# Attention block with row maxima from half-precision q and k, and the projected chunk ahead of the two weighings of its pair of steps

## The chip, the cores and the metric

The kernel runs on one core of a Trainium2 chip. The metric is the device time of one execution in microseconds (us); the median of the runs counts. The engines are TensorE (PE; its weight loads have a row of their own, PEld), VectorE (DVE), ScalarE (ACT), GpSimd (POOL) and SyncE (SP, which here only issues DMAs).

## The reference, cut to what matters

Input x is 2 x 2048 x 256, with 16 heads of 64. Each half is a residual around two layer norms.

```
x = x + layernorm(attn(layernorm(x)))     # q,k,v = x@Wq+bq, x@Wk+bk, x@Wv+bv
                                          # softmax(q.k^T / 8) @ v, @ Wo + bo, add, layernorm, gamma, beta
x = x + layernorm(ffn(layernorm(x)))      # silu(x@wg^T) * (x@wu^T) @ wd^T, weights scaled by 1/127
```

All of it is in float32. The softmax subtracts each query's largest score before the exponential; any number near that maximum gives the same quotient, since it divides out.

## The kernel before, in words

Float32 accuracy comes from splitting a number into a high part and the rest, and multiplying the parts. The operands of the projections and the scores are of the type fp32r, a four-byte form that TensorE takes in one pass; those of the weighing are f16.

The attention part handles two batches of 16 heads. For each (batch, head) there are 4 blocks of 512 queries (`NB`) and 16 tiles of 128 keys (`KT`), so 64 steps a head (`STEPS`), 2048 in all. A step t on TensorE is written out in `head` of the TensorE program and does, in this order:

- **max_tile** (L726 to L736): one product of 128 queries by 512 keys into one of two banks of `ps_aux`, for a block of queries two blocks ahead, so that in steps 32 to 63 it works for the next head. It uses `q_hilo` and `k_hihi`, 128 rows deep. The query is the stationary operand; it takes every fourth column of `qA`, that is one element in 16 bytes. VectorE reads the bank with `reduce_max` (L562, `maximum`) and thereby frees it; TensorE may not write a bank before (`used`, a list of two entries in TensorE's program, holds what each bank waits for).
- **score** (L738 to L747), for step t + 6: two products into a ring of four banks, `ps_score`. The second, 65 rows deep, also subtracts the maximum. ScalarE then computes the exponential of the bank twice (L513, L514), once to f32 and once to f16.
- **weigh** (L749 to L772), after each odd step for the last two steps: 8 short f16 products a step into `ps_ctx`, with the probabilities as the stationary operand. They need the rest `p_l` = `p_f` - `p_h`, made by VectorE in steps with t % 8 in (1, 3, 5) (`low`, L579) and by GpSimd in the others (L442).
- **project** (L713 to L724), at steps 35, 41, 51 and 57: q and k of the head after next, 512 tokens at a time, in 6 products into a bank of `ps_aux`. It stands between the two weighings of its pair. ScalarE copies the bank to `qk_new` after the exponential of step t + 6 (`take_chunk`, L466), VectorE rounds that to `hi_st` at step t + 4 (`high_chunk`, L554), GpSimd makes the rest `lo_st` after step t + 6 (`low_chunk`, L424). The two-tiles-later max_tile waits for ScalarE's copy, because it takes the same bank.

Per block VectorE also reads the sums (L585, L587), divides (L593), reduces the maxima to a row (L565) and negates it (L571); per head it splits the projection's weights at step 24 (`split_w`, L541 to L545). When the four chunks are there, SP's `fill` copies them by six DMAs from `hi_st` and `lo_st` to the operands of the head after (L342). It is issued at the start of the head before the one that uses them, and its first reader is max_tile at step 32 of that head.

The walk over a batch is head pair 0 written out, then a hardware loop over the next six pairs, then the last pair written out. A prologue before each batch (normalising x, v for all heads, q and k of two heads, 32 tiles of maxima) and a feed-forward part at the end use the same engines.

Of the kernel before, what the change touches and what calls it, by code (L numbers as in the profile page):

```python
# [17 lines left out]
P = 128  # L18
# [19 lines left out]
CHUNKS_AT = (3, 9)  # L38

# [84 lines left out]
def attention(nc, x, wqk, bqk, Wv, bv, ident_in, v_scratch, scratch, Wo, shared):  # L124
# [18 lines left out]
    with ExitStack() as ctx:  # L143
# [10 lines left out]
        kB = [sb(f"k_lo_one{u}", [K + 1, S], F32R) for u in range(2)]  # L154
        qk_new = sb("qk_new", [P, BLK], F32)
# [47 lines left out]
        hi_ready = sem("hi_ready")  # L203
        staged = sem("staged")
# [117 lines left out]
        def _(sp):  # L322
# [13 lines left out]
            def fill(u, g):  # L336

                sp.wait_ge(staged, (g + 1) * NB + 1)
                for dst, src in ((qA[u][0:K], hi_st[0:K]), (qA[u][K:P], lo_st[0:K]),
                                 (kA[u][0:K], hi_st[K:P]), (kA[u][K:P], hi_st[K:P]),  # L340
                                 (qB[u][0:K], hi_st[0:K]), (kB[u][0:K], lo_st[K:P])):
                    sp.dma_start(dst.bitcast(F32), src).then_inc(slot_full, 16)  # L342

# [34 lines left out]
            def load_for_feed_forward():  # L378
# [3 lines left out]
                sp.wait_ge(slot_full, B * H * 96 + 16)  # L382
# [31 lines left out]
        def _(pool):  # L414
            pool.sem_inc(staged, 1)
            for u in range(2):
                nc.gpsimd.memset(kB[u][K:K + 1, :].bitcast(F32), 1.0).then_inc(ones_set, 1)
                pool.wait_ge(ones_set, u + 1)
# [31 lines left out]
        def _(act):  # L450
# [9 lines left out]
            def take_chunk(g, chunk, n, bank):  # L460
# [3 lines left out]
                act.wait_ge(staged, g * NB + chunk + 1)  # L464
                act.wait_ge(aux_full, n + 1)
# [64 lines left out]
        def _(dve):  # L530
            dve.sem_inc(pro_free, RING)
            dve.sem_inc(max_read, 2)
            dve.sem_inc(ev_step, 2)
# [14 lines left out]
            def high_chunk(g, chunk):  # L548

                cols = slice(chunk * BLK, (chunk + 1) * BLK)  # L550
                if chunk == 0:
                    dve.wait_ge(slot_full, g * 96 + 16)
                dve.wait_ge(qk_ready, g * NB + chunk + 1)
                nc.vector.tensor_copy(hi_w[:, cols], qk_new[:, :]).then_inc(hi_ready, 1)  # L554

# [146 lines left out]
        def _(pe):  # L702
            pe.sem_inc(pv_done, PROBS)
            pe.wait_ge(const_in, 32)
            pe.wait_ge(ones_set, 2)
# [20 lines left out]
            def max_tile(u, g, blk, kt, m, bank):  # L726

                tt, ch = divmod(kt, NB)
                if blk % 2 == 0 and kt == 0:
                    pe.wait_ge(slot_full, g * 96 + 96 + 16)  # L730
# [3 lines left out]
                q = qA[u][:, blk * BLK:(blk + 1) * BLK].rearrange("k (p t) -> k t p", t=TB)[:, tt]  # L734
                nc.tensor.matmul(ps_aux[:, bank], q, kA[u][:, ch * BLK:(ch + 1) * BLK],  # L735
# [84 lines left out]
            def head(b, i, g, u, first, last, coming, n):  # L820
# [3 lines left out]
                for t in range(STEPS):  # L824
# [18 lines left out]
                    if t % 2:  # L843
                        weigh(u, g, t - 1)
                        for chunk, number in chunks[t]:
                            project(g + u + 2, chunk, number % 2)
                        weigh(u, g, t)
# [559 lines left out]
```

## Time and profile before

| what | us |
|---|---|
| median of 3 runs | 3343.2 (3339.7 to 3346.1) |
| the profiled execution | 3347.2 |
| its span, first to last instruction | 3345.4 |
| TensorE busy / VectorE busy | 3095.9 / 2784.4 |
| ScalarE busy / GpSimd busy | 2473.8 / 2016.6 |

Busy time counts a matmul from its start to its modelled end, so matmuls that follow each other overlap in it; the rate is read from starts. The granted clock of TensorE is 0.969 of full on average: it is full (2.4 GHz) nearly everywhere in the attention part and at its lower level (1.2 GHz) in short stretches. A head whose stretch holds no jump of the hardware loop takes about 82.3 us, one with the jump a few more.

### The profile page before, as it was taken

How to read it: one execution, taken by the hardware profiler on the slowest of the kernel's cores; microseconds unless marked ns; L12 is line 12 of the kernel's file. 1: busy time of each engine (PE TensorE's matmuls, PEld its weight loads, DVE VectorE, ACT ScalarE, POOL GpSimd, SP SyncE). 2: the span in 40 equal slices, each digit the busy share in tenths (PEclk: the TensorE clock that was granted, in tenths of full speed). 3: DMA queues.
4: the chain of work that ended last, by engine and by line, in shares of the span. 5: the costliest groups of instructions: out<-in, count | busy, mean ns of one | idle time of the engine just before them, and what ended most of it. 6: DMA issues, size and time to landing. Idle time of an engine off the chain costs nothing. (4 is left out here: it accounts for less than half of the span.)

```text
span 3345.4 us, 77779 instructions
## 1 busy us (share of the span) xinstructions
PE 3095.9 (93%) x25440; PEld 2475.0 (74%) x25440; DVE 2784.4 (83%) x4983; ACT 2473.8 (74%) x4715; POOL 2016.6 (60%) x1550
## 2 busy tenths in 40 slices
PE   5899999999999999969999999999999999878897
PEld 4677777777777777757777777777777778667775
DVE  5688988888888888976888888888888889578886
ACT  3688888888888788856888787878888889733222
POOL 3577767676667666636777666766667677512232
PEclk9999999999999999989999999999999999989998
DMA  3522222222222122115122222222222222221110
GB/s 106 136 53 53 54 54 54 54 54 54 54 48 57 43 55 56 42 31 172 33 56 57 42 56 46 54 54 54 54 54 54 54 53 52 96 83 51 63 44 19
DMA packets 206585, 197.39 MB, mean 59 GB/s; under 512 B 157648, under 2 KB 180304, under 8 KB 193872
## 3 DMA queue, kind: packets, MB, share of 16 engines
q1 hardware_dynamic: 206160, 192.00, 24.7%
q8 instruction: 233, 3.82, 0.5%
q14 instruction: 192, 1.57, 0.2%
HBM read 53.16 MB, written 37.88 MB: 27 GB/s over the span
## 5 line engine op out<-in xcount | busy, mean ns | idle before, releaser
L442 POOL TENSOR_TENSOR p_l<-p_f,p_h 128x512 f16<-128x512 f32 x1280 | 1627.0, 1293 | 546.9 <-ACT p_h L514 546.1
L562 DVE TENSOR_REDUCE mx<-ps_aux 128x1 f32<-128x512 f32 x2048 | 1384.5, 684 | 289.3 <-PE ps_aux L735 258.8
L513 ACT ACTIVATE p_f<-ps_score 128x512 f32<-128x512 f32 x2048 | 1272.2, 622 | 358.7 <-PE ps_score L746 337.3
L514 ACT ACTIVATE p_h<-ps_score 128x512 f16<-128x512 f32 x2048 | 1283.0, 628 | 0.0
L735 PE MATMUL ps_aux<-k_hihi,q_hilo 128*128 128x512 f32 x2048 | 1037.5, 507 | 93.8 <-DVE mx L562 44.4
L768 PE MATMUL ps_ctx<-v_hi_one_lo,p_h 128*128 128x129 f16 x8192 | 929.2, 223 | 2.3 <-POOL p_l L442 1.5
L768 PEld LDWEIGHTS ps_ctx<-v_hi_one_lo,p_h 128*128 128x128 f16 x8192 | 609.2, 99 | 322.2 <-issue 264.2
L746 PE MATMUL ps_score<-q_hi_max,k_lo_one 65*128 65x512 f32 x2048 | 826.5, 404 | 0.0
L745 PE MATMUL ps_score<-q_hilo,k_hihi 128*128 128x512 f32 x2048 | 821.2, 401 | 3.7 <-DMA q_hi_max<-negm 3.1
L768 PE MATMUL ps_ctx<-v_hi_one_lo,p_l 128*128 128x65 f16 x8192 | 783.3, 195 | 0.0
L735 PEld LDWEIGHTS ps_aux<-k_hihi,q_hilo 128*128 128x128 f32 x2048 | 632.3, 309 | 173.1 <-DVE mx L562 69.1
L579 DVE TENSOR_TENSOR p_l<-p_f,p_h 128x512 f16<-128x512 f32 x768 | 712.6, 928 | 52.1 <-ACT p_h L514 27.1
L768 PEld LDWEIGHTS ps_ctx<-v_hi_one_lo,p_l 128*128 128x128 f16 x8192 | 642.1, 99 | 0.0
L746 PEld LDWEIGHTS ps_score<-q_hi_max,k_lo_one 65*128 65x128 f32 x2048 | 391.7, 191 | 90.5
L745 PEld LDWEIGHTS ps_score<-q_hilo,k_hihi 128*128 128x128 f32 x2048 | 413.7, 202 | 12.7 <-ACT p_h L514 6.7
L424 POOL TENSOR_TENSOR lo_st<-qk_new,hi_st 128x512 fp32r<-128x512 f32 x128 | 205.8, 1608 | 359.8 <-DVE hi_st L554 359.8
L1117 POOL TENSOR_TENSOR hTl<-late,hTh 128x512 fp32r<-128x512 f32 x48 | 63.2, 1318 | 276.5 <-ACT hTh L1069 276.4
L466 ACT ACTIVATE qk_new<-ps_aux,b_cur 128x512 f32<-128x512 f32 x128 | 88.0, 687 | 70.0 <-PE ps_aux L722 56.8
L432 POOL TENSOR_TENSOR p_f<-p_f,v_new 128x512 f32<-128x512 f32 x64 | 72.1, 1136 | 90.0 <-ACT v_new L498 89.6
L722 PE MATMUL ps_aux<-xTh,w_h 128*128 128x512 f32 x256 | 112.9, 441 | 12.6 <-DVE xTl L614 5.5
L458 ACT ACTIVATE sums<-ps_ctx 128x516 f32<-128x516 f32 x128 | 78.5, 614 | 44.8 <-PE ps_ctx L768 44.8
L585 DVE SCALAR_TENSOR_TENSOR ctx_u<-sums 128x256 f32<-128x256 f32 x128 | 99.7, 779 | 5.1 <-ACT sums L458 5.1
(122 smaller groups left out, 2538.4 us busy)
## 6 DMA issues: line engine op xcount, KB each, us to landing
k_hihi<-hi_st SPq DMA_DIRECT2D x64, 512.0 KB, 8.6
v_heads<-v_new SPq DMA_DIRECT2D x64, 258.0 KB, 2.0
v_hi_one_lo<-v_heads SPq DMA_DIRECT2D x32, 516.0 KB, 9.7
q_hilo<-hi_st SPq DMA_DIRECT2D x32, 512.0 KB, 4.4
q_hilo<-lo_st SPq DMA_DIRECT2D x32, 512.0 KB, 6.6
q_hi_max<-hi_st SPq DMA_DIRECT2D x32, 512.0 KB, 9.2
k_lo_one<-lo_st SPq DMA_DIRECT2D x32, 512.0 KB, 10.1
heads<-ctx_n SPq DMA_DIRECT2D x128, 128.0 KB, 2.0
```

The source lines that it names most:

```text
L424: nc.gpsimd.tensor_tensor(lo_w[:, cols], qk_new[:, :], hi_st[:, cols], ALU.subtract)\
L442: nc.gpsimd.tensor_tensor(p_l[:, r], p_f[:, r], p_h[:, r], ALU.subtract).then_inc(lo_pool, 1)
L513: nc.scalar.activation(p_f[:, r], ps_score[:, bank], ACT.Exp, scale=K ** -0.5)
L514: nc.scalar.activation(p_h[:, r], ps_score[:, bank], ACT.Exp, scale=K ** -0.5).then_inc(exp_done, 1)
L562: nc.vector.reduce_max(mx[:, blk % 2, tt, ch:ch + 1], ps_aux[:, bank], AX_X).then_inc(max_read, 1)
L579: nc.vector.tensor_tensor(p_l[:, r], p_f[:, r], p_h[:, r], ALU.subtract).then_inc(lo_dve, 1)
L585: nc.vector.scalar_tensor_tensor(out=ctx_u[:, :, :], in0=acc[:, :, K + 1:VW], scalar=1.0 / LO_SCALE, in1=acc[:, :, 0:K], op0=ALU.mult, op1 ...
L722: mm = nc.tensor.matmul(ps_aux[:, bank], w[:, c], t[:, c, cols], start=(m == 0), stop=(m == len(parts) - 1))
L735: nc.tensor.matmul(ps_aux[:, bank], q, kA[u][:, ch * BLK:(ch + 1) * BLK], start=True, stop=True).then_inc(aux_full, 1)
L745: nc.tensor.matmul(ps_score[:, t % RING], kA[u][:, keys], qA[u][:, cols], start=True, stop=False)
L746: nc.tensor.matmul(ps_score[:, t % RING], kB[u][:, keys], qB[u][:, cols], start=False, stop=True).then_inc(s_full, 1)
L768: mm = nc.tensor.matmul(acc[:, 0:width], p[:, r, q * P:(q + 1) * P], V[u][:, kt, 0:width], start=(kt == 0 and q % 2 == 0 and p is p_h), st ...
```

## The change

Three things are done.

1. Two new pairs of tiles, `q_half` and `k_half` (65 x 2048, f16), hold q and k of a head rounded to half precision, with a 65th row of zeros. VectorE makes the copy from `qk_new` right after the rounding to `hi_st`, into `half_st`; ScalarE waits for it before it overwrites `qk_new`; `fill` has two more DMAs, so that a fill counts 8 transfers and not 6.
2. `max_tile` multiplies these instead of `q_hilo` and `k_hihi`. The query is still every fourth column, now one element in 8 bytes.
3. `project` stands ahead of both weighings of its pair.

GpSimd has four more memsets at the very start (the rows of zeros), and TensorE waits for them with the two that are there.

```diff
+        qM = [sb(f"q_half{u}", [K + 1, S], F16) for u in range(2)]
+        kM = [sb(f"k_half{u}", [K + 1, S], F16) for u in range(2)]
+        half_st = sb("half_st", [P, S], F16)
...
+                sp.wait_ge(half_ready, (g + 1) * NB + 1)
+                for dst, src in ((qM[u][0:K], half_st[0:K]), (kM[u][0:K], half_st[K:P])):
+                    sp.dma_start(dst, src).then_inc(slot_full, 16)
...
+                nc.gpsimd.memset(qM[u][K:K + 1, :], 0.0).then_inc(ones_set, 1)
+                nc.gpsimd.memset(kM[u][K:K + 1, :], 0.0).then_inc(ones_set, 1)
...
                 act.wait_ge(staged, g * NB + chunk + 1)
+                act.wait_ge(half_ready, g * NB + chunk + 1)
                 act.wait_ge(aux_full, n + 1)
...
                 nc.vector.tensor_copy(hi_w[:, cols], qk_new[:, :]).then_inc(hi_ready, 1)
+                nc.vector.tensor_copy(half_st[:, cols], qk_new[:, :]).then_inc(half_ready, 1)
...
-                q = qA[u][:, blk * BLK:(blk + 1) * BLK].rearrange("k (p t) -> k t p", t=TB)[:, tt]
-                nc.tensor.matmul(ps_aux[:, bank], q, kA[u][:, ch * BLK:(ch + 1) * BLK],
+                q = qM[u][:, blk * BLK:(blk + 1) * BLK].rearrange("k (p t) -> k t p", t=TB)[:, tt]
+                nc.tensor.matmul(ps_aux[:, bank], q, kM[u][:, ch * BLK:(ch + 1) * BLK],
                                  start=True, stop=True).then_inc(aux_full, 1)
...
                     if t % 2:
-                        weigh(u, g, t - 1)
                         for chunk, number in chunks[t]:
                             project(g + u + 2, chunk, number % 2)
+                        weigh(u, g, t - 1)
                         weigh(u, g, t)
```

On TensorE, in the last two steps of a pair that holds a chunk, the program before reads (ps_aux is the bank of maxima and chunks, w_h and w_l the parts of the projection's weights):

```order
L745 MATMUL ps_score<-q_hilo,k_hihi 128x512 [waits exp_done]
L746 MATMUL ps_score<-q_hi_max,k_lo_one 128x512
L761 ISA
L768 MATMUL ps_ctx<-v_hi_one_lo,p_h 128x129 [waits lo_pool]
L768 MATMUL ps_ctx<-v_hi_one_lo,p_l 128x65 x2
L768 MATMUL ps_ctx<-v_hi_one_lo,p_h 128x129 x2
L768 MATMUL ps_ctx<-v_hi_one_lo,p_l 128x65 x2
L768 MATMUL ps_ctx<-v_hi_one_lo,p_h 128x129
L717 ISA
L722 MATMUL ps_aux<-xTh,w_h 128x512 [waits max_read]
L722 MATMUL ps_aux<-xTh,w_l 128x512
```

and the changed program at the same place:

```order
L748 MATMUL ps_aux<-k_half,q_half 128x512 [waits max_read]
L756 ISA
L758 MATMUL ps_score<-q_hilo,k_hihi 128x512 [waits exp_done]
L759 MATMUL ps_score<-q_hi_max,k_lo_one 128x512
L730 ISA
L735 MATMUL ps_aux<-xTh,w_h 128x512 [waits max_read]
L735 MATMUL ps_aux<-xTh,w_l 128x512
```

The chunk's six products now follow the second score, and one step's weighing no longer lies between them. On VectorE, at the step where a chunk is rounded, the program before reads (hi_st is the high part, qk_new the chunk):

```order
L562 TENSOR_REDUCE mx<-ps_aux 128x1 [waits aux_full]
L552 ISA
L553 ISA [waits slot_full]
L554 CAST hi_st<-qk_new 128x512 [waits qk_ready]
L578 ISA
L579 TENSOR_TENSOR p_l<-p_f,p_h 128x512 [waits exp_done]
```

and the changed one:

```order
L575 TENSOR_REDUCE mx<-ps_aux 128x1 [waits aux_full]
L564 ISA
L565 ISA [waits slot_full]
L566 CAST hi_st<-qk_new 128x512 [waits qk_ready]
L567 CAST half_st<-qk_new 128x512
L591 ISA
L592 TENSOR_TENSOR p_l<-p_f,p_h 128x512 [waits exp_done]
```

One more cast stands ahead of VectorE's next share of the rests.

## Rows read from the trace of the kernel before

**Rows 1.** Page, part 1: busy time, share of the span, instructions.
```profile
PE 3095.9 (93%) x25440; PEld 2475.0 (74%) x25440; DVE 2784.4 (83%) x4983; ACT 2473.8 (74%) x4715; POOL 2016.6 (60%) x1550
```
**Rows 2.** Windows: stretch, length, busy PE, PEld, DVE, ACT, POOL, clock, DMA, GB/s.
```profile
1689.77:1772.06 82.29, 80.86 (x733) 64.78 (x731) 73.83 (x116) 70.43 (x137) 57.98 (x44) 1.00 0.27 54
2025.63:2114.76 89.13, 82.96 (x733) 66.15 (x731) 72.41 (x116) 70.57 (x137) 56.78 (x44) 0.96 0.25 51
```
**Rows 3.** Timeline of TensorE over one pair of steps: start us, duration us, line.
```profile
1001.87 0.59 PE L735 MATMUL ps_aux<-k_hihi,q_hilo 128*128 128x512 f32 x1
1002.30 0.39 PE L745 MATMUL ps_score<-q_hilo,k_hihi 128*128 128x512 f32 x1
...
1002.77 0.40 PE L735 MATMUL ps_aux<-k_hihi,q_hilo 128*128 128x512 f32 x1
1003.01 0.40 PE L745 MATMUL ps_score<-q_hilo,k_hihi 128*128 128x512 f32 x1
...
1003.48 0.23 PE L768 MATMUL ps_ctx<-v_hi_one_lo,p_h 128*128 128x129 f16 x1
...
1004.17 0.60 PE L735 MATMUL ps_aux<-k_hihi,q_hilo 128*128 128x512 f32 x1
```
**Rows 4.** Groups of weight loads in the head 1689.77 to 1772.06: busy us, mean ns.
```profile
L735 PEld LDWEIGHTS ps_aux<-k_hihi,q_hilo 128*128 128x128 f32 x64 | 19.8, 309 | 3.7 <-DVE mx L562 2.2
L768 PEld LDWEIGHTS ps_ctx<-v_hi_one_lo,p_h 128*128 128x128 f16 x258 | 19.1, 98 | 10.0 <-issue 8.9 <-POOL p_l L442 1.1
L745 PEld LDWEIGHTS ps_score<-q_hilo,k_hihi 128*128 128x128 f32 x64 | 12.8, 200 | 0.0
...
L722 PEld LDWEIGHTS ps_aux<-xTh,w_h 128*128 128x128 f32 x8 | 1.5, 189 | 0.4 <-DVE mx L562 0.2
```
**Rows 5.** Timeline of TensorE at a chunk behind a weighing.
```profile
1112.14 0.48 PE L722 MATMUL ps_aux<-xTh,w_h 128*128 128x512 f32 x1
1112.46 0.39 PE L722 MATMUL ps_aux<-xTh,w_l 128*128 128x512 f32 x1
```
**Rows 6.** Groups of VectorE and TensorE's maxima in the head 1689.77 to 1772.06.
```profile
L562 DVE TENSOR_REDUCE mx<-ps_aux 128x1 f32<-128x512 f32 x65 | 43.9, 683 | 8.3 <-PE ps_aux L735 7.2
...
L735 PE MATMUL ps_aux<-k_hihi,q_hilo 128*128 128x512 f32 x64 | 32.4, 507 | 1.3 <-DVE mx L562 1.3
...
L579 DVE TENSOR_TENSOR p_l<-p_f,p_h 128x512 f16<-128x512 f32 x24 | 23.1, 961 | 0.0
...
L585 DVE SCALAR_TENSOR_TENSOR ctx_u<-sums 128x256 f32<-128x256 f32 x4 | 3.2, 807 | 0.0
...
L593 DVE TENSOR_TENSOR ctx_n<-ctx_u,rden 128x256 f32<-128x256 f32 x4 | 3.1, 772 | 0.0
```
**Rows 7.** Timeline of VectorE, two operations back to back.
```profile
1769.75 0.68 DVE L562 TENSOR_REDUCE mx<-ps_aux 128x1 f32<-128x512 f32 x1
1770.35 1.19 DVE L579 TENSOR_TENSOR p_l<-p_f,p_h 128x512 f16<-128x512 f32 x1
1771.46 0.68 DVE L562 TENSOR_REDUCE mx<-ps_aux 128x1 f32<-128x512 f32 x1
```
**Rows 8.** Timeline of VectorE, the same operation short and long.
```profile
624.63 0.42 DVE L554 CAST hi_st<-qk_new 128x512 fp32r<-128x512 f32 x1
...
624.96 0.68 DVE L579 TENSOR_TENSOR p_l<-p_f,p_h 128x512 f16<-128x512 f32 x1
...
626.93 1.53 DVE L579 TENSOR_TENSOR p_l<-p_f,p_h 128x512 f16<-128x512 f32 x1
```
**Rows 9.** Timeline of TensorE just behind the loop's jump.
```profile
638.70 0.81 PE L735 MATMUL ps_aux<-k_hihi,q_hilo 128*128 128x512 f32 x1 [2.85 <-issue]
```
**Rows 10.** Page, part 6: DMA issues, KB each, us to landing; the last of a fill.
```profile
k_lo_one<-lo_st SPq DMA_DIRECT2D x32, 512.0 KB, 10.1
```
**Rows 11.** One line's instructions (GpSimd's first memsets): ns min/median/max, first and last start.
```profile
L417 POOL MEMSET k_lo_one<- x2: 1797/1797/1797, 0.8 to 2.7; 1x2048 f32 x2
```
**Rows 12.** Timeline of TensorE's first products.
```profile
12.27 1.94 PE L790 MATMUL ps_score<-identity,x_all 128*128 128x128 f32 x8 [12.27 <-DVE x_all L114]
```

More of the change, by code:

```diff
@@ L38 @@
 CHUNKS_AT = (3, 9)
+FILLS = 8
 def lo_on_dve(t):
@@ L203, in attention @@
         hi_ready = sem("hi_ready")
+        half_ready = sem("half_ready")
         staged = sem("staged")
@@ L381, in load_for_feed_forward @@
                     sp.wait_ge(ctx_out[u], H * NB // 2 * 16 + 16)
-                sp.wait_ge(slot_full, B * H * 96 + 16)
+                sp.wait_ge(slot_full, B * H * FILLS * 16 + 16)
                 sp.dma_start(c_first, c_src)\
@@ L417, in _ @@
                 nc.gpsimd.memset(kB[u][K:K + 1, :].bitcast(F32), 1.0).then_inc(ones_set, 1)
-                pool.wait_ge(ones_set, u + 1)
+                nc.gpsimd.memset(qM[u][K:K + 1, :], 0.0).then_inc(ones_set, 1)
+                nc.gpsimd.memset(kM[u][K:K + 1, :], 0.0).then_inc(ones_set, 1)
+                pool.wait_ge(ones_set, 3 * u + 3)
             def low_chunk(g, chunk):
@@ L532, in _ @@
             dve.sem_inc(max_read, 2)
+            dve.sem_inc(half_ready, 1)
             dve.sem_inc(ev_step, 2)
@@ L551, in high_chunk @@
                 if chunk == 0:
-                    dve.wait_ge(slot_full, g * 96 + 16)
+                    dve.wait_ge(slot_full, g * FILLS * 16 + 16)
                 dve.wait_ge(qk_ready, g * NB + chunk + 1)
                 nc.vector.tensor_copy(hi_w[:, cols], qk_new[:, :]).then_inc(hi_ready, 1)
+                nc.vector.tensor_copy(half_st[:, cols], qk_new[:, :]).then_inc(half_ready, 1)
             def maximum(hd, blk, kt, n, m, bank):
@@ L704, in _ @@
             pe.wait_ge(const_in, 32)
-            pe.wait_ge(ones_set, 2)
+            pe.wait_ge(ones_set, 6)
             used = []
@@ L729, in max_tile @@
                 if blk % 2 == 0 and kt == 0:
-                    pe.wait_ge(slot_full, g * 96 + 96 + 16)
+                    pe.wait_ge(slot_full, (g + 1) * FILLS * 16 + 16)
                 pe.wait_ge(*used.pop(0))
                 used.append((max_read, m + 3))
-                q = qA[u][:, blk * BLK:(blk + 1) * BLK].rearrange("k (p t) -> k t p", t=TB)[:, tt]
-                nc.tensor.matmul(ps_aux[:, bank], q, kA[u][:, ch * BLK:(ch + 1) * BLK],
+                q = qM[u][:, blk * BLK:(blk + 1) * BLK].rearrange("k (p t) -> k t p", t=TB)[:, tt]
+                nc.tensor.matmul(ps_aux[:, bank], q, kM[u][:, ch * BLK:(ch + 1) * BLK],
                                  start=True, stop=True).then_inc(aux_full, 1)
```

## The prediction

> **What bounds the kernel now.** The first view is part 1 of the page [rows 1]: TensorE is busy 93% of the span, VectorE 83%, ScalarE 74%, GpSimd 60%. That names TensorE, but a busy TensorE need not be at its rate, so the second view is one head cut out by windows [rows 2]. The stretch from 1689.77 to 1772.06 runs from step 24 of one head to step 24 of the next at the full clock and with no jump of the loop: 82.29 us, TensorE idle 1.4 of it, VectorE 8.5, ScalarE 11.9. The third view, the timeline of TensorE over a pair of steps, gives the rate by starts [rows 3]. The pair lasts 4.17 - 1.87 = 2.30 us: the first max_tile 0.43 (1.87 to 2.30), the second 0.24 (2.77 to 3.01), four scores of 0.235 (2.30 to 2.77 is two), and 0.69 for the 16 products of the two weighings. The reader is to see that two equal products take 0.43 and 0.24. The first follows a product of 129 columns, and the groups of weight loads say why that matters [rows 4]: the load of max_tile takes 309 ns, that of a score 200, of a chunk 189, of a weighing 98. Behind a product of 0.24 us even 309 ns is hidden; behind one of about 0.06 us it isn't. A chunk behind a weighing shows the same with a shorter load: its first product takes 0.32 (112.14 to 112.46) where its kind takes 0.23 [rows 5], 0.09 more. So what is exposed goes with the load's length: 0.19 at 309 ns, 0.09 at 189 ns, and by the same line nothing at 98 ns, which is what the weighings' own products show.
>
> Last, the waits: in that head VectorE waited 7.2 us for TensorE's maxima, TensorE 1.3 us for VectorE [rows 6]. TensorE sets the pace, and VectorE is the one close behind.
>
> **The change part by part.** The sum is made against the profiled execution's 3347.2 us (span 3345.4), 4.0 above the median of 3343.2.
>
> *The first maximum of a pair.* It takes 0.43 now. With f16 operands its load should fall to near 98 ns and vanish behind the last weighing product. Its own 512 columns at 2.4 GHz are 0.213; the f16 products show start to start what they cost above their columns (0.69 for 16 products, 1552 columns, which are 0.647: 0.003 each), so 0.216. Gain 0.21. The trace has no strided f16 load: the nearest rows are the contiguous f16 load (98) and the strided fp32r load over the contiguous one, 309 over 189 to 200, a factor of 1.6. At 1.6 x 98 = 157 ns some 0.06 would stay exposed, and the gain be 0.15. I take 0.21, since the stride in bytes is half of the one that costs, and keep 0.15 for the range.
>
> The Trainium skill, "SBUF — State Buffer", in the note on cachelines in "Door 1", has it that reads hit full speed with two or more elements in a 16-byte line, so that f32 may not step by four elements but a 2-byte type may. This agrees with 309 against 200 for f32, no run here yet shows the f16 side, and by it the gain is the full 0.21.
>
> *The second maximum.* It goes from 0.24 to 0.216, gain 0.02. The score behind each maximum has a load of 200 ns, which must hide under 0.216 where it had 0.24; it fits by the line above. Together the pair goes from 2.30 to 2.07.
>
> *Chunks.* Four a head. Ahead of the weighings a chunk follows a score, so its first load is hidden: 0.09 each, 0.36 a head. What is queued behind it: both weighings come 1.4 us later than the second score instead of one of them. Moving it 0.35 earlier also asks for its bank earlier; the reduction that frees it is that of the pair's first maximum, issued 0.22 + 0.47 + 0.22 + 0.47 = 1.38 before, and ends 1.25 after that at best, so any lateness of VectorE shows here. The copy by ScalarE that frees the bank again for the second maximum of the next pair now has 0.69 + 0.22 + 0.47 = 1.38 us where it had 0.35 + 0.43 + 0.47 = 1.25.
>
> *TensorE's own floor.* A head now: 32 x 2.30 + 4 x (0.32 + 5 x 0.23) = 79.5. Afterwards: 32 x 2.07 + 4 x 1.38 = 71.8. If TensorE stayed the bound, that would be 7.7 a head.
>
> *VectorE.* It gains a cast a chunk. The cast to `hi_st` has 0.42 us and lets the next operation start after 0.33 [rows 8]; the f16 one reads the same tile. I take 0.33, with half of it and 0.68 (a two-input operation of the size [rows 8]) as ends: 1.3 a head (0.7 to 2.7). Its whole work by starts: a reduction 0.60 (1769.75 to 1770.35), a `p_l` 1.11 where it is listed with 1.19 [rows 7], so 0.08 less than its duration. 64 x 0.60 = 38.4; 24 x (0.961 - 0.08) = 21.1; the rest is 6.3 for sums and divisions [rows 6], 1.7 for four casts [rows 8] and some 5 for the short ones and the split of the weights, 13 by durations in 21 operations, 11.4 by starts. Floor 70.9 now, 72.2 with the casts; by busy time as it stands it would be 73.8 + 1.3 = 75.1. So VectorE, at 72.2 to 75.1, passes TensorE's 71.8. **This is what is late next.**
>
> *The head afterwards.* The two halves differ. Steps 0 to 31 have no chunk: TensorE 33.1, VectorE half of 59.5 plus 4.2 of block work plus 1.6 for the split: 35.6. VectorE bounds. Steps 32 to 63: TensorE 33.1 + 5.6 = 38.7, VectorE 29.8 + 4.2 + 2.6 (casts) = 36.6. TensorE bounds. Sum 74.3. On top come the moments when the other is late, because two banks hold only some 0.8 us of slack (a reduction ends 1.25 after its product starts, the bank is wanted 2.07 after) against lumps of 0.8 (sums), 0.8 (division) and two casts in a row. Today's head loses 82.3 - 79.5 = 2.8 above its floor, mostly to such lumps. Between 0 and 2.8 I take 1.7: 76.0 a head, 6.3 less than 82.3.
>
> *The others.* ScalarE has 70.4 of busy time a head and GpSimd 58.0 [rows 2], under 76. The two f16 transfers add to a fill whose last transfer lands after 10.1 us [rows 10]; its first reader is 32 steps (some 38 us) later. SP's wait for `half_ready` stands behind the one for `lo_st`, which GpSimd makes out of the same chunk and later, so `load_v` and `load_w` behind it on SP's queue wait no longer. Without that cover a late fill would cost a head a few us. The memsets: six of at most 1.80 us in a row from 0.8 end at 11.7 [rows 11], the first product starts at 12.27 [rows 12]; uncovered, 7 us once. The pause behind the jump, 2.85 us with no wait named [rows 9], and the lower clock after it (the second head of rows 2 takes 89.13 at 0.96) are fixed and stay: 10 heads have them, before and after.
>
> *Sum.* 28 heads have all the work: 28 x 6.3 = 176. Heads 14 and 30 have no chunks: VectorE-bound at 2 x 34 + 1.6 = 69.6 plus 0.8, against 32 x 2.30 + 1.5 = 75.1; 5 each. Heads 15 and 31 make maxima in half of their steps: 3 each. The 64 maxima of the prologues follow fp32r products and gain 0.02 each, 1 in all. The feed-forward part is unchanged. 176 + 16 + 1 = 193: 3347.2 - 193 = 3154, or **3150** on the scale of the median.
>
> **The rivals.**
>
> *A. TensorE stays the bound.* VectorE's lumps cost no more than today, because its operations run closer together under pressure: TensorE's gain of 7.7 a head comes in full. For it: VectorE's 8.5 us idle. Against: its floor of 72.2. 28 x 7.7 + 22 = 238: 3105.
>
> *B. VectorE saturates early.* Its work doesn't shrink to the starts' sum but stays at the 75.1 of busy time, or the cast and the strided load take their upper ends, and the lumps add 3: 78.5 a head, gain 3.8. 28 x 3.8 + 10 = 116: 3227. For it: the longer `p_l` of 1.53 beside 0.68 [rows 8], which show that VectorE's speed isn't its own.
>
> *C. The load isn't what is exposed*, but the passage from an f16 product to an fp32r one; it then reappears at the score behind the first f16 maximum. Only 2 x 0.02 a pair and the chunks' 0.09 would stay: 1.6 a head, of which VectorE's casts may take up to 1.3; at 1.0 a head, 3343 - 28 = 3315. Against it: two fp32r loads of different length have different exposures [rows 4, 5]. The Trainium skill, "TensorE: Matmul & The Clock Gate", section "LDWEIGHTS (loading the stationary operand)", puts a load at its number of columns over 1.2 GHz, whatever the type; by that the f16 load of 128 columns would be no shorter than the old, and C would hold. The rows 309, 200 and 98 for 128 columns each speak against it.
>
> *D. Slower: VectorE and GpSimd block each other.* `p_l` on VectorE takes 0.68 alone and 1.53 in other places, 0.961 in the mean [rows 6, 8]. If at the denser pace all 24 of a head took 1.53, VectorE would need 72.2 + 24 x 0.57 = 85.9, that is 3.6 above today's head: 3343 + 28 x 3.6 = 3444. It decides from a mean of 1.38 on, where VectorE's floor reaches 82.3. Against it: GpSimd's share only goes from 58/82.3 = 70% to 58/76 = 76%, which by proportion lifts the 0.28 above 0.68 by 0.02. The Trainium skill, "SBUF — State Buffer", "SBUF: two separate sides", describes an exclusive port pair which an operation of VectorE with two inputs or in its fast copy mode shares with GpSimd; the two durations agree.
>
> **How the numbers follow.** Forecast (3110 to 3195) 0.60; A 0.16; B 0.15; C 0.05 (its half nearer to no change 0.02); D 0.04. The range holds the forecast, A and most of B: 3095 to 3240. About 0.2% is what a measurement of this kernel can tell from no change. Faster: 0.60 + 0.16 + 0.15 + 0.03 = 0.94; same 0.02; slower 0.04.
>
> **What would show it.** Right: the group of max_tile's loads at about 100 ns, its products 0.22 apart from the scores in both places of a pair, the chunk's first product at 0.23, pairs of 2.07 where VectorE has no lump. VectorE busy over 93% of a head, TensorE's waits for it up from 1.3 us to several, a head near 76.0 and the same pause behind the jump. Wrong: loads of 150 ns or more, 0.4 from the first maximum to its score (C), a mean of `p_l` over 1.1 us (D), or ScalarE without idle time in a head, which no term here has.

## The result, and the profile after

The changed kernel takes 3504.0 us in the median of 4 runs (3499.0 to 3512.6), beside 3344.4 for the kernel before on the same chip: a ratio of 1.0483 [1.0469, 1.0497]. It is slower by 160 us; forecast was 3150. The profiled execution took 3512.6 us, with a span of 3509.8 and a mean granted clock of 0.94, where the span before was 3345.4 and the clock 0.969. Of the ten runs of one kernel below (x2) two lay far above the others, at 4101.6 and 6445.2 us; they are slow runs, and neither its ratio nor the time given for it counts them.

Part 1 of its page, which answers [rows 1], and the costliest groups of part 5 that answer [rows 6]: busy us and mean ns, then the idle time ahead.

```profile
PE 3062.3 (87%) x25440; PEld 2168.8 (62%) x25440; DVE 2920.7 (83%) x5111; ACT 2473.5 (70%) x4715; POOL 2031.8 (58%) x1554
...
L592 DVE TENSOR_TENSOR p_l<-p_f,p_h 128x512 f16<-128x512 f32 x768 | 825.6, 1075 | 45.9 <-ACT p_h L525 28.1
L748 PE MATMUL ps_aux<-k_half,q_half 65*128 65x512 f16 x2048 | 840.7, 411 | 164.9 <-DVE mx L575 104.3
L748 PEld LDWEIGHTS ps_aux<-k_half,q_half 65*128 65x128 f16 x2048 | 233.9, 114 | 527.1 <-DVE mx L575 252.8
L434 POOL TENSOR_TENSOR lo_st<-qk_new,hi_st 128x512 fp32r<-128x512 f32 x128 | 179.1, 1399 | 438.4 <-DVE hi_st L566 438.4
```

The reader is to see three things. TensorE's busy share fell from 93% to 87%, and no other engine's rose. The load of a maximum is short, 114 ns where it was 309 [rows 4], so the step that the forecast turned on did happen. And VectorE gained 136 us of busy time. The 128 new casts of 0.42 are 54; the same 768 `p_l` grew by 113, from 712.6 us in all to 825.6 (neighbours that overlap take some of the sum back).

The waits of the whole span (engine, tile and line, what it waited for: us in all, times, longest):

```profile
PE ps_aux L748 <- DVE mx L575: 104.3, 227, 3.7
PE ps_aux L735 <- DVE mx L575: 93.4, 95, 1.2
DVE w_h L555 <- DMA w_raw<-in_wqk: 40.1, 25, 2.5
PE ps_score L758 <- DMA q_hi_max<-negm: 38.5, 23, 7.7
```

The kernel before had these:

```profile
PE ps_aux L735 <- DVE mx L562: 44.4, 52, 3.4
PE ps_score L745 <- DMA q_hi_max<-negm: 3.1, 1, 3.1
```

So TensorE waits far more for VectorE's maxima (197.7 us in the first two rows; before, 44.4 at the maxima and 3.5 at the chunks), above all at the chunks (L735). VectorE's wait for `w_raw` is new, and TensorE's for the row of maxima has grown from one of 3.1 us to 23 with 38.5. The windows over two heads, in the columns of [rows 2], show the price and the lower clock that comes with it. The second holds the loop's jump; before, such heads took 82.29 and 89.13.

```profile
1868.40:1956.72 88.32, 79.77 (x733) 55.30 (x730) 78.03 (x121) 70.65 (x137) 58.15 (x44) 0.96 0.27 55
1956.72:2051.18 94.46, 83.27 (x732) 57.93 (x729) 76.50 (x120) 70.63 (x137) 56.98 (x44) 0.91 0.27 55
```

By the record of the granted clock, TensorE stood at 1.2 GHz for 211 us of the span before, in 30 stretches, and for 426 us now, in 65.

### The profile page after: what moved, and what is told of

It is laid out like the page before. It is cut to its first block and busy times, and to the rows that moved or that the text cites. A ratio compares the mean times of both kernels' runs of the same rounds, so it can differ in the third digit from the quotient of the medians.

```text
span 3509.8 us, 78104 instructions
## 1 busy us (share of the span) xinstructions
PE 3062.3 (87%) x25440; PEld 2168.8 (62%) x25440; DVE 2920.7 (83%) x5111; ACT 2473.5 (70%) x4715; POOL 2031.8 (58%) x1554
## 5 line engine op out<-in xcount | busy, mean ns | idle before, releaser
L452 POOL TENSOR_TENSOR p_l<-p_f,p_h 128x512 f16<-128x512 f32 x1280 | 1662.6, 1319 | 616.4 <-ACT p_h L525 616.4
L575 DVE TENSOR_REDUCE mx<-ps_aux 128x1 f32<-128x512 f32 x2048 | 1366.0, 682 | 278.6 <-PE ps_aux L748 261.6
L758 PE MATMUL ps_score<-q_hilo,k_hihi 128*128 128x512 f32 x2048 | 1219.6, 595 | 41.0 <-DMA q_hi_max<-negm 38.5
L748 PE MATMUL ps_aux<-k_half,q_half 65*128 65x512 f16 x2048 | 840.7, 411 | 164.9 <-DVE mx L575 104.3
L592 DVE TENSOR_TENSOR p_l<-p_f,p_h 128x512 f16<-128x512 f32 x768 | 825.6, 1075 | 45.9 <-ACT p_h L525 28.1
L781 PE MATMUL ps_ctx<-v_hi_one_lo,p_l 128*128 128x65 f16 x8192 | 801.2, 197 | 0.0
L781 PEld LDWEIGHTS ps_ctx<-v_hi_one_lo,p_l 128*128 128x128 f16 x8192 | 659.4, 101 | 0.0
L748 PEld LDWEIGHTS ps_aux<-k_half,q_half 65*128 65x128 f16 x2048 | 233.9, 114 | 527.1 <-DVE mx L575 252.8
L434 POOL TENSOR_TENSOR lo_st<-qk_new,hi_st 128x512 fp32r<-128x512 f32 x128 | 179.1, 1399 | 438.4 <-DVE hi_st L566 438.4
L735 PE MATMUL ps_aux<-xTh,w_h 128*128 128x512 f32 x256 | 119.0, 465 | 99.4 <-DVE mx L575 93.4
L735 PEld LDWEIGHTS ps_aux<-xTh,w_h 128*128 128x128 f32 x256 | 51.1, 200 | 152.6 <-DVE mx L575 136.5
```

The source lines that it names most:

```text
L434: nc.gpsimd.tensor_tensor(lo_w[:, cols], qk_new[:, :], hi_st[:, cols], ALU.subtract)\
L452: nc.gpsimd.tensor_tensor(p_l[:, r], p_f[:, r], p_h[:, r], ALU.subtract).then_inc(lo_pool, 1)
L575: nc.vector.reduce_max(mx[:, blk % 2, tt, ch:ch + 1], ps_aux[:, bank], AX_X).then_inc(max_read, 1)
L592: nc.vector.tensor_tensor(p_l[:, r], p_f[:, r], p_h[:, r], ALU.subtract).then_inc(lo_dve, 1)
L735: mm = nc.tensor.matmul(ps_aux[:, bank], w[:, c], t[:, c, cols], start=(m == 0), stop=(m == len(parts) - 1))
L748: nc.tensor.matmul(ps_aux[:, bank], q, kM[u][:, ch * BLK:(ch + 1) * BLK], start=True, stop=True).then_inc(aux_full, 1)
```

## Two mechanisms in the trace

**The order at the port.** Here is a place where a chunk is rounded, on VectorE, GpSimd and TensorE (start us, duration us):

```profile
1177.94 0.42 DVE L566 CAST hi_st<-qk_new 128x512 fp32r<-128x512 f32 x1
1178.28 0.42 DVE L567 CAST half_st<-qk_new 128x512 f16<-128x512 f32 x1
1178.44 1.40 POOL L434 TENSOR_TENSOR lo_st<-qk_new,hi_st 128x512 fp32r<-128x512 f32 x1 [3.58 <-DVE hi_st L566]
1178.61 1.78 DVE L592 TENSOR_TENSOR p_l<-p_f,p_h 128x512 f16<-128x512 f32 x1
1180.32 1.27 DVE L575 TENSOR_REDUCE mx<-ps_aux 128x1 f32<-128x512 f32 x2
1181.05 0.50 PE L735 MATMUL ps_aux<-xTh,w_h 128*128 128x512 f32 x1 [1.15 <-DVE mx L575]
```

and such a place in the kernel before, VectorE and then GpSimd:

```profile
1118.22 0.42 DVE L554 CAST hi_st<-qk_new 128x512 fp32r<-128x512 f32 x1
1118.55 0.69 DVE L579 TENSOR_TENSOR p_l<-p_f,p_h 128x512 f16<-128x512 f32 x1
```
```profile
1118.72 1.67 POOL L424 TENSOR_TENSOR lo_st<-qk_new,hi_st 128x512 fp32r<-128x512 f32 x1 [1.79 <-DVE hi_st L554]
```

The rounding to `hi_st` releases GpSimd's `lo_st`, which starts 0.50 us after the rounding did. In the kernel before, VectorE's `p_l` had started by then, 0.33 after: it took 0.69, and `lo_st` took 1.67, where it takes 1.40 when it is first. With a second cast in between, GpSimd starts first, and `p_l`, which starts 0.17 later, ends 0.55 after `lo_st` does: 1.78. Over the 112 places where a `p_l` stands right behind the casts its mean went from 0.72 to 1.78, while the other 656 kept theirs within 0.02 (0.96), and the mean of `lo_st` fell from 1608 to 1399 ns. 112 x 1.06 = 119 us accounts for the 113 by which all `p_l` grew. The Trainium skill, "SBUF — State Buffer", "SBUF: two separate sides", has it that the engine that starts first holds the shared port pair for its whole instruction; the trace agrees, with 1.78 for the `p_l` that starts second and 0.69 for the one that starts first.

**SP's queue.** The timeline of SP in the changed kernel, at the head of a head (start us, duration us of the issue):

```profile
693.53 2.28 SPq L347 DMA_DIRECT2D q_hi_max<-hi_st  x1
695.86 2.49 SPq L347 DMA_DIRECT2D k_lo_one<-lo_st  x1
698.49 2.07 SPq L350 DMA_DIRECT2D q_half<-half_st  x1
700.60 1.66 SPq L350 DMA_DIRECT2D k_half<-half_st  x1
702.48 0.64 SPq L357 DMA_DIRECT2D v_hi_one_lo<-v_heads  x1
703.40 4.51 SPq L339 DMA_DIRECT2D w_raw<-in_wqk  x1
708.05 0.53 SPq L363 DMA_DIRECT2D q_hi_max<-negm  x1
```

Behind it VectorE, then TensorE:

```profile
710.97 0.83 DVE L555 CAST w_h<-w_raw 128x256 fp32r<-128x256 f32 x1 [1.80 <-DMA w_raw<-in_wqk]
```
```profile
711.24 0.50 PE L758 MATMUL ps_score<-q_hilo,k_hihi 128*128 128x512 f32 x1 [1.48 <-DMA q_hi_max<-negm]
```

The two new transfers hold SP's queue for 4.0 us. `w_raw` and the row of maxima, issued behind them, land too late: VectorE stands 1.80 us, TensorE 1.48. In the kernel before the same queue had a margin: `w_raw` was issued at 743.93, had landed 7.9 us later and was taken at 753.43 without a wait, 9.5 us after its issue; here it is taken as soon as it has landed, 7.57 us after its issue. So the margin was 1.6 us, and the new transfers take 4.0.

## The experiments

All ratios are against the kernel before on the same chip, with the 95% interval. Differences called "by the ratio" are on 3344. Each kernel has a short name in brackets, by which it is called again.

**Which part costs?** Four kernels take the change apart. The first (e1) is the changed kernel with `project` back between the two weighings:

```diff
                     if t % 2:
+                        weigh(u, g, t - 1)
                         for chunk, number in chunks[t]:
                             project(g + u + 2, chunk, number % 2)
-                        weigh(u, g, t - 1)
                         weigh(u, g, t)
```

> Half-precision maxima and casts as in the changed kernel, but the chunk between the two weighings as before. Theory V (VectorE's lateness is the cause: the casts and longer rests make TensorE wait, and its clock drops in the waits; the chunk's place matters little): 3440 to 3500. Theory P (the chunk's place is the cause: its bank is asked for earlier, with no weighing to cover the wait): 3180 to 3260, about what was forecast. If both are needed, something between.

Measured: 3457.2, 1.0343 [1.0326, 1.0360]. The second (e2) is the kernel before with the reverse edit alone.

```diff
                     if t % 2:
-                        weigh(u, g, t - 1)
                         for chunk, number in chunks[t]:
                             project(g + u + 2, chunk, number % 2)
+                        weigh(u, g, t - 1)
```

> The kernel before with the chunk ahead of both weighings, nothing else. Theory V: 3330 to 3360, since TensorE is behind VectorE here and the bank is mostly free. Theory P: 3420 to 3500.

Measured: 3346.8, 1.0005 [0.9995, 1.0014]. The chunk's new place costs nothing there, and 47 us in the changed kernel: not the place costs, but what it meets. The third (e4) is the kernel before with the casts, the two transfers and their waits, while the maxima still come from `q_hilo` and `k_hihi`; the f16 copies are used by nobody.

```diff
+                nc.vector.tensor_copy(half_st[:, cols], qk_new[:, :]).then_inc(half_ready, 1)
...
+                act.wait_ge(half_ready, g * NB + chunk + 1)
...
+                sp.wait_ge(half_ready, (g + 1) * NB + 1)
+                for dst, src in ((qM[u][0:K], half_st[0:K]), (kM[u][0:K], half_st[K:P])):
+                    sp.dma_start(dst, src).then_inc(slot_full, 16)
```

> The kernel before with the cast on VectorE, the two more DMAs of a fill and the waits for them, but the maxima from the four-byte operands and the old place of the chunk. It prices the preparation alone. Theory V: TensorE still sets the pace, VectorE had 8.5 us idle a head and takes 1.3 more: 3345 to 3390. Theory P: 3345 to 3355.

Measured: 3498.1, 1.0459 [1.0442, 1.0477]. Nearly the whole loss, with no f16 maximum in it, and far above both ranges expected. In its groups VectorE's `p_l` and GpSimd's `lo_st` read as in the changed kernel:

```profile
L592 DVE TENSOR_TENSOR p_l<-p_f,p_h 128x512 f16<-128x512 f32 x768 | 816.0, 1063 | 45.7 <-issue 25.0 <-ACT p_h L525 20.2
...
L434 POOL TENSOR_TENSOR lo_st<-qk_new,hi_st 128x512 fp32r<-128x512 f32 x128 | 179.5, 1403 | 431.6 <-DVE hi_st L566 431.6
```

The fourth (x3) is the kernel before with the two transfers alone, from a `half_st` that is set to zero once; no casts.

```diff
+                sp.wait_ge(half_ready, 1)
+                for dst, src in ((qM[u][0:K], half_st[0:K]), (kM[u][0:K], half_st[K:P])):
+                    sp.dma_start(dst, src).then_inc(slot_full, 16)
```

> The kernel before with only the two more DMAs of a fill (their source is set once at the start, no copy is made, so what they carry isn't used; maxima from the four-byte operands). Theory S: at the slower pace the weights still come about in time, 3344 to 3360. If SP's queue costs as much here as in the changed kernel: 3400 or more. Theory O: the rest of the cast-only kernel's 154 us is the casts' and stays away here.

Measured: 3412.5, 1.0200 [1.0183, 1.0217]. Two transfers that nobody needs cost 2.0%, and bring the two waits of SP's queue with them:

```profile
DVE w_h L554 <- DMA w_raw<-in_wqk: 17.9, 24, 1.1
...
PE ps_score L756 <- DMA q_hi_max<-negm: 13.7, 19, 5.4
```

By the ratio, and in this order: transfers +67, casts +87 (e4 over x3), f16 maxima -39 (e1 under e4), the chunk's place +47. Together that is 162, the whole of 1.0483. Taken off in another order the parts are of another size: in the changed kernel the order of the casts alone is worth 110 us and the queue 119, as the next runs show.

**Is it the casts' work or their order?** The changed kernel, with the two casts in the other order (x1); the work is the same.

```diff
+                nc.vector.tensor_copy(half_st[:, cols], qk_new[:, :]).then_inc(half_ready, 1)
                 nc.vector.tensor_copy(hi_w[:, cols], qk_new[:, :]).then_inc(hi_ready, 1)
-                nc.vector.tensor_copy(half_st[:, cols], qk_new[:, :]).then_inc(half_ready, 1)
```

> The changed kernel with the two casts of a chunk in the other order: first the half-precision copy, then the rounding to hi_st that lets GpSimd begin. Theory O (order of arrival: with the copy behind the rounding, GpSimd's lo_st begins first and VectorE's next p_l waits for all of it, 1.78 us for 0.69, in 112 places): p_l behind the casts back at 0.69, lo_st back at 1.6, and 3504 - 112 x 1.09 = 3380, between 3360 and 3410. Theory N (it is the number of casts, 128 x 0.336 us, that makes VectorE late, the long p_l being a consequence of a denser pace): 3485 to 3510, p_l unchanged.

Measured: 3393.9, 1.0154 [1.0136, 1.0172]: 110 us less for the order of two lines. VectorE in a place of a chunk, and its group of `p_l`:

```profile
1131.46 0.42 DVE L566 CAST half_st<-qk_new 128x512 f16<-128x512 f32 x1
1131.80 0.42 DVE L567 CAST hi_st<-qk_new 128x512 fp32r<-128x512 f32 x1
1132.13 0.69 DVE L592 TENSOR_TENSOR p_l<-p_f,p_h 128x512 f16<-128x512 f32 x1
...
L592 DVE TENSOR_TENSOR p_l<-p_f,p_h 128x512 f16<-128x512 f32 x768 | 648.7, 845 | 43.5 <-issue 21.9 <-ACT p_h L525 21.4
```

The `p_l` is back at 0.69, and TensorE's waits for maxima fell from 197.7 us to 94.7 (66.6 and 28.1). The first mechanism is shown: nothing else in that kernel differs. The gain isn't all at the 112 places, though. All `p_l` together fell by 177 us, of which these places are 122; the group even stands below the kernel before (712.6). Most of the rest is at the `p_l` of steps 45 and 61, each the next one behind such a place. They took 1.50 in the changed kernel, 1.46 before, and take 0.73 to 0.76 here: VectorE's then starts some 0.02 us after GpSimd's own `p_l` and no longer 0.15 after it.

**The copy on ScalarE** (e3). ScalarE makes the f16 copy out of the bank, ahead of its copy to `qk_new`, and VectorE none.

```diff
+                nc.scalar.activation(half_st[:, chunk * BLK:(chunk + 1) * BLK], ps_aux[:, bank], ACT.Identity,
+                                     bias=b_cur[:, 0:1]).then_inc(half_ready, 1)
...
-                nc.vector.tensor_copy(half_st[:, cols], qk_new[:, :]).then_inc(half_ready, 1)
```

> The changed kernel with the half-precision copy made by ScalarE out of the bank (one more activation of about 0.5 us a chunk) and not by VectorE. Theory V: VectorE loses 128 casts of 0.336 us = 43 us of work, at places where TensorE waits for it, so 3400 to 3470. Theory P: within 20 of 3504.

Measured: 3374.3, 1.0083 [1.0066, 1.0099]. It is below both ranges, so the cast cost more than its own length; but all of VectorE's added work is gone and it is still slower than before. Its waits name what is left:

```profile
PE ps_score L760 <- DMA q_hi_max<-negm: 44.4, 26, 7.4
...
DVE w_h L558 <- DMA w_raw<-in_wqk: 42.3, 25, 2.3
```

**SP's queue.** First the small edit, on e3 (x2): SP's block with `fill` and `load_v` moves from ahead of `load_w` to behind it, so that `w_raw` is issued first.

> The kernel with the copy on ScalarE (3374) and, on SP's queue, the load of the next weights issued ahead of the fill and not behind it. Theory S (the two transfers push the weights and the next maxima's transfer 3.6 us back on SP's queue: VectorE waits 42 us for w_raw, TensorE 44 for the maxima, and the clock drops at that place in every head): no wait for w_raw, lower-clock time down from 381 towards 220, 3230 to 3310. Theory K (the half-precision products themselves make the clock drop or don't come faster): 3350 to 3380 with as much time at the lower clock.

Measured: 3357.5 in the median of eight runs (3342 to 3368), 1.0034 [1.0018, 1.0050]. The wait for `w_raw` is gone, but the one for the row of maxima grew to 52.2 us: the queue is as long as it was. By time (3350 to 3380) and by 392 us at the lower clock this is what theory K forecast; the run after next decides against it. The same kernel with the chunk in its old place (x4):

> The kernel of the run before last (copy on ScalarE, weights' load first) with the chunk between its two weighings again. It tells what the chunk's place is worth once VectorE isn't late: by the prediction's term 0.09 a chunk, 12 us slower than that one; if the early chunk waits for its bank, equal or faster.

Measured: 3373.7, 1.0090 [1.0066, 1.0115]; its ten runs go from 3353 to 3393. The new place gains some 19 us here by the ratio, of the size of the scatter, where it cost 47 us in the changed kernel. The whole queue was late, so it was then spread over the head. At the head's start SP issues `w_raw` and the two f16 transfers, which have a semaphore of their own; the six of the fill come behind the first row of maxima, `load_v` behind the second.

```diff
+                    fill_half(1 - u, g + u + 1)
...
+                    if j == 0 and not (last and u == 1):
+                        fill(1 - u, g + u + 1)
+                    if j == 1 and not (last and u == 1):
+                        load_v(b, i + u + 1, 1 - u)
```

TensorE's waits follow: for the f16 pair at step 32, for the six transfers at the first score. The kernel with ScalarE's copy and this queue (y1):

> The copy on ScalarE, and SP's queue spread over the head: weights first, then only the two half-precision transfers at the head's start; the six of the fill behind the first maxima row, v behind the second. TensorE waits for the half-precision pair at step 32 and for the six at the first score of the next head. Theory S (what is left above the forecast is the wait for the maxima row, 52 + 13 us, and the lower clock it brings, 392 us against 211, each worth half its length): no such wait, and 3361 - 60 - 60 to 90 = 3210 to 3250. Theory K (the clock drops because of the half-precision products): the waits go, the lower-clock time stays near 390, and 3300 or more.

Measured: 3279.2, 0.9808 [0.9792, 0.9825], 95 us less than e3. The time lies between the two ranges. Neither of the two waits is in its list, and the time at 1.2 GHz fell from 381 us to 231 with all the f16 products still there, which refutes theory K. The changed kernel with the queue's edit alone, VectorE's casts as they are (y4):

> The changed kernel with only SP's queue spread; both casts stay on VectorE in their order. Additive theory: the queue is worth what it is worth in the pair of kernels with the copy on ScalarE (3374 against the run beside this), so about 3504 - 130 = 3370. If VectorE's lateness at the chunks hides the queue's waits: above 3430.

Measured: 3387.7, 1.0128 [1.0111, 1.0145], 119 us less by the ratio. With the casts swapped too (z3):

> The changed kernel with SP's queue spread and the two casts on VectorE swapped, so half copy first, then the rounding. By the order theory 112 x 1.09 us of VectorE's time go, which was worth 110 us alone: 3388 - 110 = 3278. If VectorE's own 128 x 0.336 us weigh as much as its lateness did before: 3300 to 3330.

Measured: 3279.2, 0.9810 [0.9794, 0.9826]. Swap (3.3 points) and queue (3.6 points) come to 6.8 together before rounding, and both at once give 6.7: they add up, so they are two causes and not one. This is the change as it was meant, with the same work on the same engines. It gains 64 us.

The chunk's place again, now in the kernel without the waits (y1 with the old order, called y2):

> The same with the chunk between its two weighings. With nothing else late, the prediction's term says 128 x 0.09 = 12 us slower; a bank that the early chunk must wait for would make this one equal or faster.

Measured: 3301.2, 0.9876 [0.9859, 0.9892]. Here the new place gains 22 us; in the changed kernel it cost 47. The forecast's 0.36 a head would be 10.

**What still separates 3279 from 3150?** ScalarE's copy in y1 holds the bank for one operation more. In the next kernel (z1) it writes `qk_new` first and makes the f16 copy from that.

```diff
-                nc.scalar.activation(half_st[:, chunk * BLK:(chunk + 1) * BLK], ps_aux[:, bank], ACT.Identity,
-                                     bias=b_cur[:, 0:1]).then_inc(half_ready, 1)
...
+                nc.scalar.activation(half_st[:, chunk * BLK:(chunk + 1) * BLK], qk_new[:, :], ACT.Copy)\
+                    .then_inc(half_ready, 1)
```

> As the kernel with the copy on ScalarE and SP's queue spread (3279), but ScalarE first writes qk_new, which frees the bank and starts VectorE, and makes the half-precision copy from qk_new behind that. If ScalarE's hold of the bank is the rest (TensorE waits 72 us on its load row for qk_new): 3279 - 128 x 0.2 to 0.5 = 3215 to 3255. If VectorE is: 3265 to 3285.

Measured: 3253.4, 0.9734 [0.9718, 0.9750]: the bank's hold was worth 25 us. Next VectorE's share of the rests, two of eight steps and not three, GpSimd taking the third (z2 on y1, z5 on z1, w1 on the kernel before):

```diff
-    return t % 8 in (1, 3, 5)
+    return t % 8 in (1, 5)
```

> As the 3279 kernel, but VectorE makes the rests p_l of two steps in eight and not of three, GpSimd of six. VectorE's work falls by 8 x 0.9 = 7 us a head, GpSimd's rises by 8 x 1.29 = 10 to about 67 of 80. If VectorE's work is what is left over: 3150 to 3230. If GpSimd then holds the weighings up, or something else binds: 3270 or more.

Measured, in y1: 3216.7, 0.9610 [0.9593, 0.9627], 66 us less by the ratio. In z1:

> The first and the second of this call together. If both terms are real: 3120 to 3200. If GpSimd binds, no better than the first.

Measured: 3190.1, 0.9545 [0.9527, 0.9563]. And in the kernel before, nothing else changed:

> The kernel before, with VectorE making the rests of two steps in eight. If TensorE bounds the kernel before, only VectorE's lumps get shorter: 3310 to 3344. If VectorE was the bound all along: 3220 to 3280.

Measured: 3283.6, 0.9816 [0.9799, 0.9832]. The 62 us are there in the kernel before as well, in which VectorE idled 8.5 us of a head. A head without the jump takes 79.97 us (656.73 to 736.70) and not 82.24, and TensorE's waits at L735 fell from 44.4 us to 12.7. The rests that stay on VectorE take no less than before (940 ns against 928), so the gain is the work taken from VectorE and not less strife at the port. One rest in eight, in z1 (w2):

```diff
-    return t % 8 in (1, 3, 5)
+    return t % 8 in (1,)
```

> The 3190 kernel with VectorE making the rests of one step in eight, GpSimd of seven. GpSimd then has 56 x 1.2 + 6 = 73 us a head of some 77. If VectorE's work still binds: 3150 to 3180. If GpSimd or TensorE with ScalarE does: 3190 or more.

Measured: 3181.7, 0.9515 [0.9499, 0.9531], the fastest kernel here. Part 1 of its page:

```profile
PE 2918.7 (92%) x25440; PEld 2111.9 (67%) x25440; DVE 2432.1 (77%) x4471; ACT 2524.1 (79%) x4843; POOL 2509.5 (79%) x2066
```

The engines other than TensorE are even now. The last step gave only 0.3 points; the time falls between the two ranges, so it doesn't tell which engine binds.

**Rows of the product.** In y1, both operands of the maxima 64 rows deep (y7), without the row of zeros, which adds nothing to a product:

```diff
-                q = qM[u][:, blk * BLK:(blk + 1) * BLK].rearrange("k (p t) -> k t p", t=TB)[:, tt]
-                nc.tensor.matmul(ps_aux[:, bank], q, kM[u][:, ch * BLK:(ch + 1) * BLK],
+                q = qM[u][0:K, blk * BLK:(blk + 1) * BLK].rearrange("k (p t) -> k t p", t=TB)[:, tt]
+                nc.tensor.matmul(ps_aux[:, bank], q, kM[u][0:K, ch * BLK:(ch + 1) * BLK],
```

> The first kernel of this call with half-precision products 64 rows deep, without the row of zeros. If the depth doesn't matter: equal. If a product in half of the array costs a changeover against its neighbours of 65 and 128 rows, the pair of steps goes above 2.13 us by up to 4 x 0.06, and the time up by up to 250; if it lets products overlap, down.

Measured: 4045.4, 1.2097 [1.2077, 1.2118], three times the worst that was expected. Its timeline of TensorE at the full clock, and the row of its page that gives the granted clock in 40 slices:

```profile
906.00 0.40 PE L760 MATMUL ps_aux<-k_half,q_half 64*128 64x512 f16 x1
906.34 0.50 PE L772 MATMUL ps_score<-q_hilo,k_hihi 128*128 128x512 f32 x1
906.68 0.40 PE L773 MATMUL ps_score<-q_hi_max,k_lo_one 65*128 65x512 f32 x1
907.01 0.40 PE L760 MATMUL ps_aux<-k_half,q_half 64*128 64x512 f16 x1
...
PEclk8689978879695969998999959597887969999998
```

Products start 0.33 to 0.34 apart where some 0.23 is usual; a pair takes 2.73 us. And whole heads ran at 1.2 GHz, with pairs of 4.73, 1133 us of it in the span and 231 in y1. Behind each of the ten jumps of the loop the clock fell, as it does in y1, but it stayed low for 85 to 89 us. Why, the runs don't tell.

## Why the prediction was wrong

The forecast was 3150 and 3504 was measured. 225 us of that distance are two terms that it put at nothing: a queue of transfers and the order of two casts (3504 to 3279, z3). The other 129 are there without them: at the full clock a head of z3 without the jump takes 80.45 us and not 76.0, which over 28 heads is 125.

**The load: right.** It forecast loads near 98 ns and a vanished exposure; 114 ns were measured, and the first maximum no longer takes 0.43. The prediction cited the Trainium skill, "SBUF — State Buffer", the note on cachelines in "Door 1", for full speed with two or more elements in a 16-byte line: 309 ns against 200 with one (f32) and 114 against 98 with two (f16) bear it out nearly. Rival C would have left the first maximum at 0.4 and is refuted, but a part of what it spoke of is there (next point).

**The pair: mis-sized by 0.07.** The prediction put the first maximum at 0.216 and left the scores at 0.235. One undisturbed pair of steps on TensorE, up to the start of the next, to be read against [rows 3]:

```profile
1888.64 0.38 PE L748 MATMUL ps_aux<-k_half,q_half 65*128 65x512 f16 x1
1888.67 0.59 PE L758 MATMUL ps_score<-q_hilo,k_hihi 128*128 128x512 f32 x1
1889.09 0.40 PE L759 MATMUL ps_score<-q_hi_max,k_lo_one 65*128 65x512 f32 x1
1889.34 0.41 PE L748 MATMUL ps_aux<-k_half,q_half 65*128 65x512 f16 x1
1889.39 0.59 PE L758 MATMUL ps_score<-q_hilo,k_hihi 128*128 128x512 f32 x1
1889.82 0.40 PE L759 MATMUL ps_score<-q_hi_max,k_lo_one 65*128 65x512 f32 x1
1890.06 0.23 PE L781 MATMUL ps_ctx<-v_hi_one_lo,p_h 128*128 128x129 f16 x1
...
1890.72 0.22 PE L781 MATMUL ps_ctx<-v_hi_one_lo,p_h 128*128 128x129 f16 x1
1890.78 0.38 PE L748 MATMUL ps_aux<-k_half,q_half 65*128 65x512 f16 x1
```

and, in the kernel before, the last product of the weighings ahead of the first maximum of [rows 3]:

```profile
1001.84 0.22 PE L768 MATMUL ps_ctx<-v_hi_one_lo,p_h 128*128 128x129 f16 x1
```

The pair takes 1890.78 - 1888.64 = 2.14, not 2.07. A maximum and the score behind it take 0.45 (1888.64 to 1889.09) and 0.48, which a split of 0.216 and 0.235 would put at 0.451: the start of the score behind an f16 product isn't 0.216 after it, it is listed 0.03 to 0.05 after, with a duration of 0.59, so only the sum can be read. Of the excess 0.03 is in the second couple and 0.03 in the weighings, which take 0.72 (1890.06 to 1890.78) where the prediction kept 0.69. That second part was hidden in the rows before: there the first maximum, an fp32r product behind an f16 one, is listed 0.03 after the last weighing product started (1001.84, 1001.87), now 0.06 (1890.72, 1890.78), so 0.03 of the 0.43 wasn't the maximum's to lose. The excess is 32 x 0.065 = 2.1 us a head, up to 60 in all where TensorE sets the pace. What makes the 0.03 of the second couple wasn't tried.

**"The two f16 transfers add to a fill [...] its first reader is 32 steps (some 38 us) later": the wrong neighbour.** The step looked at the fill's reader and at what SP waits for, and said that `load_v` and `load_w` wait no longer. It left out the time that the queue itself needs to issue them, 4.0 us, ahead of `w_raw` and the row of maxima. The row of 10.1 us [rows 10] showed how slow the fill already was, but the margin of `w_raw` was never read. Worth 67 us (x3) to 119 (y4 against the changed kernel).

**VectorE's cast at 0.33: right as a duration, wrong as a cost.** It takes 0.34. But it stands between `hi_st`, which releases GpSimd, and a `p_l` that needs the same port, and costs 1.06 us more by that. The prediction had this very pair of durations in [rows 8], 0.68 beside 1.53, and rival D on it; but D asked whether a denser pace would lengthen all 24 `p_l` of a head to a mean over 1.38. It took 4 a head, by order and not by pace, and the measured mean in the head at 1868.40 is 26.9 / 24 = 1.12, just over the 1.1 that the prediction had named as D's sign. D was right in its sign, engines and port, and wrong in its place and its trigger.

**"TensorE sets the pace": half true.** In the kernel before VectorE idled 8.5 us of a head and still, one `p_l` of three moved away is worth 62 us (w1) and brings a head to 79.97, near the 79.5 that the prediction reckoned for TensorE alone. So VectorE already cost 2.3 us a head. The term that was too small is the 1.7 us on top of the floor of 74.3: with both mechanisms out of the way a head takes 80.45 (z3) or 80.05 (y1), not 76.0. By the prediction's own halves, with 2.14 for the pair, the floor is 35.6 + 39.8 = 75.4, so in y1 4.6 lie on top. Of these, 0.9 is ScalarE's hold of the bank (z1, 25 us over 28 heads); with a third fewer rests on VectorE as well a head takes 77.0, at 3190 in all (z5). That with two banks it is VectorE's longest lump between two maxima that counts, and not its share, fits this, but no run changed the length of a lump and left the work as it was.

**The clock: said to stay, didn't.** The prediction called the lower clock behind the jump fixed, and so it was, but it put no other stretch beside it. In the changed kernel 53 stretches at 1.2 GHz begin between 180 and 3000 us, 20 before, and 49 of the 53 begin within 4 us behind a pause of TensorE of 0.4 us or more. Not every wait brings one: behind the 1.48 us at 711.24 the clock stays full to the end of the head, which takes 85.55 us (709.05 to 794.60). The 215 us more of such time are up to 107 us of the loss, if TensorE does half its work in them. They went with the waits (x3 292 us, y1 231), so they are taken here as part of the waits' price; no run changed the clock alone.

**The chunk's place: right in sign, once nothing waits.** The prediction noted that the chunk asks for its bank 1.38 us after a maximum that VectorE frees after 1.25, "so any lateness of VectorE shows here". With `p_l` of 1.78 at that very place it showed: 93.4 us of waits at L735 where the old place has 61.7 (e1), and 47 us of time. With nothing late it gains 22 us (y1 against y2), twice the 10 of the forecast.

## What to carry to other kernels

A short instruction put between a release and the next user of a shared port cost three times its own length here: after each edit look at which of two engines now starts first, and put the release last. A DMA that nobody waits for still takes its queue's time; before adding one, read the issue times of what stands behind it and the margin of its reader. An engine's idle share says nothing of its lumps: move one piece of its work away and measure, before taking another engine as the bound.

## What the runs showed of the hardware

- Two transfers of 64 partitions, 256 KB each, took SP 2.07 and 1.66 us to issue, and the loads behind them came late; two unused ones cost 2.0% of the kernel.
- The f16 weight load that takes every fourth column took 114 ns, the contiguous one 98; in f32 309 and 200.
- With 64-row products between products of 65 and 128 rows the starts were 0.33 to 0.34 us apart, some 0.1 more than with 65 rows, and the clock stayed at 1.2 GHz for whole heads; the kernel took 766 us more.
- The order of two casts of 0.42 us, nothing else, was worth 110 us of 3504.
- Of 53 stretches at 1.2 GHz in the changed kernel 49 began within 4 us behind a pause of TensorE of 0.4 us or more, but a pause of 1.48 us at 711.24 brought none.
